# Attention on one core: the maximum products of a key tile issued as four row tiles beside the value products, the row of maxima built in the bank of the sums, and four scores in a row

## The reference, cut to what matters

```python
scores = jnp.einsum('bqhd,bkhd->bhqk', q, k) / np.sqrt(hd).astype(np.float32)
attn = jax.nn.softmax(scores, axis=-1)
out = jnp.einsum('bhqk,bkhd->bqhd', attn, v).reshape(B, L, D)
```

## Time and profile before

| | |
|---|---|
| median of 3 runs | 5264.52 us (5264.1 to 5265.49) |
| profiled execution | 5257.78 us, its span 5255.9 us |
| mean granted TensorE clock | 0.965 |
| attention, from its first rough product to its last totals | 1790.55 to 3985.15 us |
| 2800 to 3300 us, busy | PE 481.27, DVE 362.96, POOL 277.31, ACT 300.60 us |

### The profile page before, as it was taken

The page is one execution under the profiler, slowest core; times in us unless marked ns, Lnnn a source line. Parts: engine busy times, 40 slices in busy tenths (PEclk is TensorE's granted clock), DMA queues, the critical chain, the costliest instruction groups (busy, mean ns, idle before and its releaser), DMA issues. The chain is left out here.

```text
span 5255.9 us, 83572 instructions
## 1 busy us (share of the span) xinstructions
PE 4717.2 (90%) x25792; PEld 3011.7 (57%) x25792; DVE 3750.7 (71%) x5321; ACT 2358.7 (45%) x3683; POOL 2560.1 (49%) x1341
## 2 busy tenths in 40 slices
PE   6689999968888799999999999999996775999999
PEld 6678888846666433333333333333333664888888
DVE  6667777667787677777777777777774886677776
ACT  4433333322222255565656556565653343333332
POOL 2334444345565455555555555555554554344443
PEclk9999999989999799999999999999997886999999
DMA  4465555334444422222222232222214554555552
GB/s 136 139 198 179 172 176 161 119 135 159 153 144 140 133 51 64 63 64 64 64 58 57 63 64 64 62 64 64 64 37 129 169 160 139 177 178 168 173 175 91
DMA packets 431929, 613.85 MB, mean 117 GB/s; under 512 B 188288, under 2 KB 189568, under 8 KB 431808
## 3 DMA queue, kind: packets, MB, share of 16 engines
q1 hardware_dynamic: 390848, 545.67, 36.8%
q0 software_dynamic: 40960, 66.65, 4.0%
HBM read 452.44 MB, written 178.33 MB: 120 GB/s over the span
## 5 line engine op out<-in xcount | busy, mean ns | idle before, releaser
L1468 POOL TENSOR_TENSOR att_pairsum<-att_p,att_p 128x1024 f32<-128x1024 f32 x512 | 1203.1, 2369 | 994.5 <-ACT att_p L1486 994.5
L1540 DVE TENSOR_REDUCE att_halves<-att_mx 128x2 f32<-128x1024 f32 x1024 | 1211.2, 1221 | 534.3 <-PE att_mx L1579 531.1
L1486 ACT ACTIVATE att_p<-att_st 128x512 f32<-128x512 f32 x2048 | 1183.5, 597 | 869.1 <-PE att_st L1601 831.2
L1601 PE MATMUL att_st<-att_q,att_k 128*128 128x512 f32 x2048 | 960.3, 494 | 48.0 <-ACT att_p L1486 46.5
L1601 PEld LDWEIGHTS att_st<-att_q,att_k 128*128 128x128 f32 x2048 | 372.7, 187 | 825.7 <-issue 409.3
L1611 PE MATMUL att_op<-att_p,att_v 128*32 128x512 f32 x4096 | 549.0, 608 | 1.1 <-ACT att_p L1486 1.0
L1579 PE MATMUL att_mx<-att_k,att_q 32*128 32x512 f32 x2048 | 520.0, 503 | 27.7 <-DMA att_v<-v 15.1
L845 DVE TENSOR_TENSOR e_w<-e_raw,e_w 128x2048 fp32r<-128x2048 f32 x192 | 439.3, 2290 | 10.0 <-ACT e_w L840 6.1
L863 ACT ACTIVATE e_sg<-e_gp 128x324 f32<-128x324 f32 x256 | 113.3, 443 | 630.9 <-PE e_up L176 630.9
L840 ACT ACTIVATE e_w<-e_raw 128x2048 fp32r<-128x2048 f32 x192 | 366.4, 1909 | 56.1 <-DMA e_raw<-in_w_gate 48.1
L899 DVE SCALAR_TENSOR_TENSOR e_xg<-e_yp,e_meta,e_xg 108x512 f32<-108x512 f32 x192 | 144.2, 751 | 314.9 <-PE e_yp L176 314.9
(11 more groups left out here) (147 smaller groups left out, 9176.0 us busy)
## 6 DMA issues: line engine op xcount, KB each, us to landing
e_raw<-in_w_gate SPq DMA_DIRECT2D x64, 1024.0 KB, 5.6
e_raw<-in_w_up SPq DMA_DIRECT2D x64, 1024.0 KB, 9.5
e_raw<-in_w_down SPq DMA_DIRECT2D x64, 1024.0 KB, 5.8
att_q<-q SPq DMA_DIRECT2D x192, 256.0 KB, 4.1
att_k<-k SPq DMA_DIRECT2D x256, 128.0 KB, 5.8
r_x<-in_x SPq DMA_DIRECT2D x16, 1024.0 KB, 6.0
x<-r_base SPq DMA_DIRECT2D x16, 1024.0 KB, 9.4
qkv_x<-x SPq DMA_DIRECT2D x16, 1024.0 KB, 5.6
```

The costliest lines, as they stand in the source:

```text
L1468: nc.gpsimd.tensor_tensor(out=pairsum[h][g % 2][:, :], in0=pr[h][2 * g % RING][:, :], in1=pr[h][(2 * g + 1) % RING][:, :], op=ALU.add).the ...
L1486: nc.scalar.activation(pr[h][kt % RING][:, c * HALF:(c + 1) * HALF], st[c][:, :], ACT.Exp, scale=SCALE).then_inc(s_exp, 1)
L1540: nc.vector.tensor_reduce(out=halves[:, n // 2, n % 2, :], in_=mx[n % 2][:, :, :], axis=AX.X, op=ALU.max).then_inc(s_max, 1)
L1601: nc.tensor.matmul(st[c][:, :], kst[b][:, h, kt * P:(kt + 1) * P], qst[b][:, h, c * HALF:(c + 1) * HALF], start=True, stop=True).then_inc( ...
```

## The change

The maximum products of a whole query tile (both heads, both key halves) become one group of four matmuls on four different 32-row strips of the array, R of the new kernel. They write the four banks of a single `mx`, where two buffers of two banks were. For that two new operands are loaded, `mq` (q's high part twice) and `mk` (k's high part by halves). DVE reduces all four banks in one instruction, into `big` directly, so the combination of the halves goes. R stands once at the head of each key tile, directly ahead of P, and the four scores follow each other with nothing between. `row` writes to `zp` and stands in kt = 4 behind P; its copies are two halves each on DVE and ACT. `copy_z` comes one step earlier. The rough products go two steps further ahead: five query tiles of the pair after the next are in the tail of a step (FIRST = 5, TURN = 3).

```diff
-    ROUGH = ((1, 1, 1), (1, 0, 1), (1, 1, 1), (1, 0, 1), (1, 1, 1), (0, 0, 0), (0, 0, 1), (1, 0, 1))
-    TURN = KT - 2
+    TURN = 3
+    ROW = TURN + 1
+    FIRST = KT - TURN
+        mq = [sb(f"mq{b}", [P, L], F32R) for b in range(DEPTH)]
+        mk = [sb(f"mk{b}", [P, HALF], F32R) for b in range(DEPTH)]
-        mx = S.pair(ps, "mx", [P, 2, HALF])
+        mx = ps("mx", [P, 2, 2, HALF])
...
+                for c in range(2):
+                    rows = slice(2 * c * HD, 2 * (c + 1) * HD)
+                    sp.dma_start(mq[b][rows, :].bitcast(F32), q_in[0, src[0], :]).then_inc(s_in[b], 16)
+                    sp.dma_start(mk[b][rows, :].bitcast(F32), k_in[0, src[0], half(c)]).then_inc(s_in[b], 16)
...
# ACT
-                nc.scalar.activation(qst[b][3 * HD:4 * HD, 1, :],
-                                     mx[1][2 * HD:3 * HD, :, :].rearrange("p c q -> p (c q)"),
-                                     ACT.Copy).then_inc(s_rowq[1], 1)
+                for c in range(2):
+                    nc.scalar.activation(qst[b][3 * HD:4 * HD, 1, half(c)], zp[tile(1, c), :],
+                                         ACT.Copy).then_inc(s_rowq[1], 1)
-                        if last and (kt, x) == (3, 0):
+                        if last and (kt, x) == (2, 2):
                             copy_z(*last)
-                        if left and (kt, x) == (TURN, 3):
+                        if left and (kt, x) == (ROW, 2):
                             copy_row(*ahead(i, b, 1))
...
# DVE
+            def maxima(i, b, qt):
+                dve.wait_ge(s_mx, KT * p + qt + 1)
+                nc.vector.tensor_reduce(out=big[:, :, qt], in_=mx[:, :, :, :].rearrange("p h c k -> p h (c k)"),
+                                        axis=AX.X, op=ALU.max).then_inc(s_max, 1)
...
             def step(i, b, left):
                 if left:
-                    maxima(*ahead(i, b, 1))
+                    for qt in range(FIRST, KT):
+                        maxima(*ahead(i, b, 1), qt)
+                    split(*ahead(i, b, 1))
+                for qt in range(FIRST):
+                    if left >= 2:
+                        maxima(*ahead(i, b, 2), qt)
+                    if left and qt == ROW - TURN - 1:
+                        copy_row(*ahead(i, b, 1))
...
# PE
+            def rough(i, b, qt):
+                pe.wait_ge(s_max, KT * p + qt)
+                for c in range(2):
+                    for h in range(2):
+                        rows = slice((2 * c + h) * HD, (2 * c + h + 1) * HD)
+                        last = nc.tensor.matmul(mx[:, h, c, :], mq[b][rows, qt * P:(qt + 1) * P], mk[b][rows, :],
+                                                start=True, stop=True)
                 last.then_inc(s_mx, 1)
```

More of the change, by code:

```diff
@@ L1346, in attention @@
     SCALE = 1.0 / float(HD) ** 0.5
-    NM = 2 * KT
     CH = 4 * KT
@@ L1365, in attention @@
         pairsum = [S.pair(sb, f"pairsum{h}", [P, L]) for h in range(2)]
-        halves = sb("halves", [P, KT, 2, 2])
         big = sb("big", [P, 2, KT])
@@ L1397, in attention, with tile, half @@
         N_OUT = 4
-        N_IN = 3 + 5 + 1
-        KBLK = ((0, 1, 0), (1, 0, 0))
+        N_IN = 3 + 3 + 2 + 2 + 1
+        def tile(h, c):
+            return slice((2 * h + c) * HD, (2 * h + c + 1) * HD)
+        def half(c):
+            return slice(c * HALF, (c + 1) * HALF)
         def ahead(i, b, k):
@@ L1533, in _, with split @@
             nc.vector.tensor_copy(identb[:, :], ident[:, :]).then_inc(s_identb, 1)
-            def maxima(i, b):
+            def maxima(i, b, qt):
                 p = DEPTH * i + b
[L1538 to L1547, removed]
+                dve.wait_ge(s_mx, KT * p + qt + 1)
+                if qt == 0:
+                    dve.wait_ge(s_mlo, p)
+                nc.vector.tensor_reduce(out=big[:, :, qt], in_=mx[:, :, :, :].rearrange("p h c k -> p h (c k)"),
+                                        axis=AX.X, op=ALU.max).then_inc(s_max, 1)
+            def split(i, b):
+                p = DEPTH * i + b
+                dve.wait_ge(s_max, KT * (p + 1))
+                dve.wait_ge(s_row, p)
+                nc.vector.tensor_tensor(out=parts[:, :, :, 0], in0=big[:, :, :], in1=big[:, :, :],
+                                        op=ALU.max).then_inc(s_mhi, 1)
                 dve.wait_ge(s_mhi, p + 1)
@@ L1550, in maxima, with copy_row @@
                                         op=ALU.subtract).then_inc(s_mlo, 1)
-                dve.wait_ge(s_row, p + 1)
-                nc.vector.tensor_copy(qst[b][3 * HD:4 * HD, 0, :],
-                                      mx[1][3 * HD:4 * HD, :, :].rearrange("p c q -> p (c q)")).then_inc(s_rowq[0], 1)
+            def copy_row(i, b):
+                dve.wait_ge(s_row, DEPTH * i + b + 1)
+                for c in range(2):
+                    nc.vector.tensor_copy(qst[b][3 * HD:4 * HD, 0, half(c)], zp[tile(0, c), :]).then_inc(s_rowq[0], 1)
             def step(i, b, left):
                 if left:
-                    maxima(*ahead(i, b, 1))
-            maxima(0, 0)
+                    for qt in range(FIRST, KT):
[6 more added lines that the diff above has]
+                        copy_row(*ahead(i, b, 1))
+            for qt in range(KT):
+                maxima(0, 0, qt)
+            split(0, 0)
+            copy_row(0, 0)
+            for qt in range(FIRST):
+                maxima(0, 1, qt)
             rounds_by(DEPTH, dve, NP, step)
@@ L1566, in _ @@
             pe.wait_ge(s_identb, 1)
-            def rough(i, b, n):
+            def rough(i, b, qt):
                 p = DEPTH * i + b
-                qt, c = n // 2, n % 2
-                if n == 0:
+                if qt == 0:
                     pe.wait_ge(s_in[b], 16 * N_IN * (i + 1))
-                if n == 1:
+                pe.wait_ge(s_max, KT * p + qt)
+                for c in range(2):
                     for h in range(2):
[L1576 to L1581, removed]
+                        rows = slice((2 * c + h) * HD, (2 * c + h + 1) * HD)
+                        last = nc.tensor.matmul(mx[:, h, c, :], mq[b][rows, qt * P:(qt + 1) * P], mk[b][rows, :],
+                                                start=True, stop=True)
                 last.then_inc(s_mx, 1)
@@ L1586, in row @@
                 p = DEPTH * i + b
-                pe.wait_ge(s_max, NM * (p + 1))
+                pe.wait_ge(s_mhi, p + 1)
                 pe.wait_ge(s_mlo, p + 1)
-                for qt in range(KT):
+                pe.wait_ge(s_zo, past(p - 1))
+                for t in range(KT // 2):
                     for h in range(2):
-                        last = nc.tensor.matmul(
-                            mx[1][(3 - h) * HD:(4 - h) * HD, qt // (KT // 2), qt % (KT // 2) * P:(qt % (KT // 2) + 1) * P],
-                            parts[:, h, qt, :], identb[:, :], start=True, stop=True)
+                        for c in range(2):
+                            last = nc.tensor.matmul(zp[tile(h, c), t * P:(t + 1) * P], parts[:, h, c * (KT // 2) + t, :],
+                                                    identb[:, :], start=True, stop=True)
                 last.then_inc(s_row, 1)
@@ L1597, in scores @@
                 h, c = x // 2, x % 2
-                if kt == 0 and c == 0:
-                    pe.wait_ge(s_rowq[h], p + 1)
+                if kt == 0:
+                    pe.wait_ge(s_rowq[h], 2 * p + c + 1)
                 pe.wait_ge(s_exp, past(CH * p + 4 * kt + x - 1))
@@ L1610, in products, with totals @@
                     for c in range(2):
-                        last = nc.tensor.matmul(op[(2 * h + c) * HD:(2 * h + c + 1) * HD, :], v[b][:, kt, h, :],
-                                                pr[h][kt % RING][:, c * HALF:(c + 1) * HALF],
+                        last = nc.tensor.matmul(op[tile(h, c), :], v[b][:, kt, h, :], pr[h][kt % RING][:, half(c)],
                                                 start=kt == 0, stop=kt == KT - 1)
                 last.then_inc(s_v, 1)
-            def totals(p, g):
+            def totals(p, g, left):
                 pe.wait_ge(s_add, 2 * (NG2 * p + g) + 2)
@@ L1620, in totals @@
                     pe.wait_ge(s_zo, p)
+                    for h in range(2):
+                        pe.wait_ge(s_rowq[h], 2 * (p + (2 if left else 1)))
                 for h in range(2):
                     for c in range(2):
-                        last = nc.tensor.matmul(zp[(2 * h + c) * HD:(2 * h + c + 1) * HD, :], ones[:, :],
-                                                pairsum[h][g % 2][:, c * HALF:(c + 1) * HALF],
+                        last = nc.tensor.matmul(zp[tile(h, c), :], ones[:, :], pairsum[h][g % 2][:, half(c)],
                                                 start=g == 0, stop=g == NG2 - 1)
@@ L1633, in step @@
                 before = not isinstance(i, int) or i + b > 0
-                n = FIRST
                 for kt in range(KT):
+                    if kt < TURN and left:
```

(22 more changed lines are left out.)

14 lines of the change are left out of this document (4 added, 10 removed).

## The result

The changed kernel takes 5406.74 us (median of 4 runs, 5401.95 to 5411.03), against 5264.31 us before (median of 4 as well): a ratio of 1.0275, 95% interval 1.0261 to 1.0289. It is slower by about 142 us. The forecast was 5353, so the direction and the range of 5265 to 5470 held, and 54 us of the size are missing: the result lies outside the 40 us around the forecast that had a chance of 0.52.

The account below looks back on a forecast made before the run. PE's order bounds attention, a pair going from 33.75 to 34.83 us. Pairs +66, written-out pairs +3, last two -0.5, start +17, load +3 give +88 on 5257.8: 5346 profiled, 5353 as median; range 5265 to 5470.

Parts of the forecast that it names:

- What bounds the kernel: Attention loop: PE's order sets the time, PE being busy 481 of 500 us at full granted clock.
- A: PE's time from R to P in the new order, once per key tile: 0.43 us, range 0.23 to 0.645.
- Rival 1: R on PE: four strips don't stream together, R to P 0.645 us, +107 us, time 5459; chance 0.12.
- rival 2: R to P on PE: no shape change paid, 0.23 us, 99 us less, time 5254; chance 0.12.
- the 0.07 us a step: R on PE: streaming 1.3 times as long by the skill's four-row-tile figure, some 32 us in all.
- The copies on ACT: Copies between ACT's exponentials delay the fourth score: 0.48 us each in kt = 0 and 2, 0.96 in kt = 4.
- Step 4: Key tile kt = 4, with `row`: 5.72 us, including 0.79 because the next R waits for DVE's reduction.
- rival 3: DVE is no hold in kt = 4: up to 0.79 us a pair goes, 49 us, time 5304; chance 0.12.
- The split is hidden: DVE's split in kt = 2, after POOL's first adds: about 0.5 us, not waited for until kt = 4.
- The start: Start of attention: with one `mx`, first R to first score takes about 41 us, +17.
- The added load: Before the first R: 2560 KB to load instead of 1792, costing 0 to +6.5 us, taken as 3.
- Rival 4: The clock falls as PE is less busy: low start clock 100 us longer, some 40 us, time 5393; chance 0.06.

Follow-up runs that it names:

- Runs one to three: Against the changed kernel: DVE's row copy behind the second reduction, 5346.51 us; ACT's copies behind the fourth exponential, 5463.88; both edits together, 5162.72.

## Why the prediction was right, and where its size was off

- **What bounds the kernel, and A.** PE's order, and every piece of it, were read rightly: A is 0.44 (0.43 forecast), a step 3.53. Rival 1, strips that don't stream together, and rival 2, no price for a change of shape between R and P, both fall by the row from R to P. Nor does R stream longer for having four matmuls (0.50 us, as the two before), so nothing is seen of the 0.07 us a step that the prediction works out as an estimate. The run with R in the wait shows that the 0.43 is all exposed beside P and all hidden between the scores.
- **The copies on ACT.** 0.48 in steps 0 and 2 held. The row's copies were mis-sized: 0.96 was taken from the spacing of 512-column operations on all partitions; they start 0.62 behind the third exponential and take 1.23 until the fourth starts, so the fourth score came 1.85 after the third and not 0.49, 1.36 later than without them.
- **Step 4.** The step came to 5.54 us (5.72 forecast): `row` was shorter (0.34 to the scores instead of 0.55, and 0.45 to the copy instead of 0.66, as it now spreads over four column strips), DVE's copies and reduction took 1.43 + 2.29. The hold by DVE is 0.42 at R, not 0.79, because ACT's copies already cover the rest; rival 3, no hold at all, is half true. The errors nearly cancel, which is luck: the pair is 34.89 against 34.83.
- **The split is hidden** in step 2, at 0.23 and 0.23, as said; the run with TURN = 3 and R moved shows what it costs without that cover.
- **The start.** First R to first score 40.9 us, 41 forecast. The added load cost 5.6, in the upper part of its 0 to 6.5. I had left out that the clock's low stretch at the start (granted clock 0.50) now falls on work that DVE bounds anyway. It ends at 1844.2 us before the change and at 1845.3 after it, but the first score is at 1814.78 and at 1837.10, so 29 us of scores ran at half clock before and 8 after. That gives most of the 9.7 us back.
- **The clock** is the step that failed in size. Rival 4 had 0.06 and looked only at the mean: PE 85% busy in the last pair at a granted clock of 1.00. That was true and the wrong question. What matters is the one stretch where PE stands idle 1.35 us and then 0.36 again. It cost about 60 us, more than the whole gap between forecast and result: without it the time would have been about 5345, 8 under the forecast. The range held the result only because it reached up to 5470 for rival 1, which did not happen; that is luck. Runs one to three show it from three sides: less waiting, fewer falls; one piece of 1.71, a fall in nearly every pair; no long wait, none.

What stays open: why with the same wait of 1.35 us some pairs fall and others not, 20 of 56 in one order and 5 of 56 in a fuller one. No run varied the length of the wait by itself.

## What to carry to other kernels

When an operation is to be moved, ask which wait it fills at its old place and whether there is one at the new: the same packed group gave 5163 us beside the value products and 4962 where the engine waits anyway. Write down the longest single wait that the new order makes on TensorE, not only its busy share, since behind waits of 1.35 to 1.77 us the clock fell here, in some pairs or in all. In the changed kernel these falls cost some 60 us. And test orders of two engines together: here each alone gave -60 and +57 us, and both -244.

## What was not expected of the hardware

- The granted clock fell from 2.4 to 1.2 GHz in the step behind a single wait of 1.71 us, with PE about 85% busy over the pair, in 55 of 56 intervals; the low stretch reached 9 us (a granted clock of 0.50 from 2839 to 2848). With waits of 0.45 in each of the eight steps, and none above 0.63 in any pair of the loop, it stayed at 1.00.
- Two ACT copies of 32 partitions by 512 columns between exponentials push the next one by 1.36 us together, while a copy of 128 partitions by 512 columns pushes it by 0.48.
- A DVE reduction of 2048 columns over four banks took 2293 ns, 1221 for 1024: the second 1024 columns cost 1.07 us.
